# Self-attention heads in two row halves of TensorE, and value products in two column halves, in a decoder layer

## What is computed

```python
q = x @ W_q; k = x @ W_k; v = x @ W_v
latent = (k + v) @ W_down_kv
k_rec, v_rec = latent @ W_up_k, latent @ W_up_v      # 16 heads of 8
scores = einsum('bhqd,bhkd->bhqk', q, k_rec) / sqrt(128)
scores = scores * exp(-0.01 * |t_q - t_k|)
x = x + (softmax(scores) @ v_rec) @ W_o
```

## Time and profile before

| | us |
|---|---|
| median of 3 runs | 535.52 (535.09 to 536.34) |
| profiled execution, device time | 537.88 |
| its span, first to last instruction | 536.1 |
| PE busy | 494.6 (92%) |
| DVE busy | 361.3 (67%) |
| ACT busy | 335.9 (63%) |
| POOL busy | 170.6 (32%) |

### The profile page before, as it was taken

How to read it: one execution, slowest core, us unless ns; L and a number is a source line. 1 busy time by engine, 2 the same in 40 slices (tenths; PEclk the granted TensorE clock), 3 DMA queues, 4 the chain that set the end, 5 groups by cost and what they waited for, 6 DMA issues and landing times.

```text
span 536.1 us, 9771 instructions
## 1 busy us (share of the span) xinstructions
PE 494.6 (92%) x3480; PEld 320.3 (60%) x3480; DVE 361.3 (67%) x858; ACT 335.9 (63%) x659; POOL 170.6 (32%) x292
## 2 busy tenths in 40 slices
PE   7349899999999999997998999999999999999997
PEld 6205433333333333333545998989889898888896
DVE  6889988887878787742436447766666677664345
ACT  4635777878777777787655573837556373647521
POOL 6820023444453544334353312321322322210000
PEclk9857999999999999999898999999999999999999
DMA  8987300034003300003369633424333533400000
GB/s 238 296 253 144 74 17 3 3 76 105 2 2 90 90 2 3 2 4 117 81 187 330 176 93 109 128 61 153 94 119 94 156 97 84 149 19 1 6 6 6
DMA packets 27956, 49.22 MB, mean 92 GB/s; under 512 B 4140, under 2 KB 15860, under 8 KB 27332
## 3 DMA queue, kind: packets, MB, share of 16 engines
q1 hardware_dynamic: 27156, 47.87, 32.3%
q0 software_dynamic: 224, 0.54, 0.4%
q10 hardware_dynamic: 528, 0.18, 0.1%
HBM read 43.67 MB, written 4.72 MB: 90 GB/s over the span
## 4 chain that ended last, share of the span: by engine, by line
PE 71%; DVE 21%; issue 3%; ACT 2%; DMA 1%; POOL 1%; SPq 1%; DVEq 0%; POOLq 0%; ACTq 0%
PE banks L981 48%; PE banks L1090 12%; PE banks L1246 6%; DVE banks L807 6%; DVE logits L883 2%; PE banks L1101 2%; DVE fa L917 1%; DMA operands<-query_parts 1%; DVE fa L913 1%; DVE qc_lo L854 1%; DVE xn L927 1%; DVE f_small L910 1%; DVE fa L918 1%; PE banks L1153 1%; DVE fa L916 1%
## 5 line engine op out<-in xcount | busy, mean ns | idle before, releaser
L672 ACT ACTIVATE probs<-banks 128x512 f32<-128x512 f32 x288 | 160.2, 599 | 50.7 <-PE banks L981 45.2
L807 DVE CUSTOM_DVE_ANT_0 banks<-banks,decay 128x1024 f32<-128x1024 f32 x128 | 155.0, 1244 | 32.4 <-PE banks L981 31.7
L981 PE MATMUL banks<-operands 112*128 112x512 bf16 (+4 forms) x736 | 149.1, 333 | 21.7 <-DMA operands<-query_parts 14.8
L981 PEld LDWEIGHTS banks<-operands 115*128 115x128 bf16 (+1 forms) x736 | 55.4, 98 | 128.0 <-ACT probs L672 55.5
L981 PEld LDWEIGHTS banks<-mem,pT 128*128 128x128 f32 (+1 forms) x816 | 105.5, 191 | 7.5
L981 PE MATMUL banks<-mem,pT 128*128 128x128 f32 (+1 forms) x816 | 109.1, 275 | 0.0
L693 ACT ACTIVATE pT<-banks 128x512 f32<-128x512 f32 (+1 forms) x104 | 60.4, 580 | 52.0 <-PE banks L1246 52.0
L883 DVE CUSTOM_DVE_ANT_0 logits<-banks,mring 128x512 f32<-128x512 f32 (+1 forms) x85 | 56.5, 667 | 27.4 <-PE banks L981 18.6
L535 POOL TENSOR_SCALAR_AFFINE_SELECT probs<-probs 128x128 f32<-128x128 f32 x128 | 37.1, 293 | 111.0 <-ACT probs L672 109.2
L1090 PE MATMUL banks<-probs,v_ext 128*32 128x512 f32 x512 | 68.7, 609 | 0.1
L527 POOL TENSOR_SCALAR mring<-mring 128x1024 f32<-128x1024 int32 (+1 forms) x46 | 43.8, 952 | 62.0 <-DMA mring<-in_mask_BxSxS_ik 60.0
(11 more groups left out here) (169 smaller groups left out, 502.1 us busy)
## 6 DMA issues: line engine op xcount, KB each, us to landing
mring<-in_mask_BxSxS_ik SPq DMA_DIRECT2D x39, 512.0 KB, 3.7
operands<-key_parts SPq DMA_DIRECT2D x24, 192.0 KB
operands<-query_parts SPq DMA_DIRECT2D x21, 192.0 KB
key_parts<-operand_parts SPq DMA_DIRECT2D x10, 256.0 KB, 3.5
mem<-in_ctx SPq DMA_DIRECT2D x3, 832.0 KB, 9.0
mask<-in_mask_BxSxS_ik SPq DMA_DIRECT2D x9, 256.0 KB, 3.0
pT<-in_mask_BxSxS_ik SPq DMA_DIRECT2D x9, 256.0 KB, 3.0
query_parts<-operand_parts SPq DMA_DIRECT2D x4, 384.0 KB, 5.1
```

Source lines behind the costliest of these rows:

```text
L672: act.activation(probs[:, to, :], PS[:, u % 3, :], ACT.Exp).then_inc(s_p, 1)
L807: dve.tensor_tensor_reduce(out=rows, in0=rows, in1=decay[:, off:off + S], scale=1.0, scalar=-3.0e38, op0=ALU.mult, op1=ALU.max, accum_out= ...
L981: return pe.matmul(o, a, b, start=start, stop=stop, skip_group_check=alone)
```

## The change

The shifted copies go: the parts are stored as the six products that count (48 rows), so that the math takes 60 rows and all with the shift 63. Heads 0 and 1 of a group lie in partitions 0 to 62, heads 2 and 3 in 64 to 126. The order of heads in a block changes, so that a score unit and the maximum half next to it in PE's order are mostly in different row halves; a maximum unit is issued as two halves around other work; the ninth score unit is issued as two halves, the second after a semaphore of the first; a value product is issued as two halves of 256 columns with a score unit between them. The spare rows' memsets now cover 128 partitions by half the columns. Stores of key parts are 3 DMAs in place of 5, of query parts 6 in place of 2, loads 2 in place of 3 each.

```diff
--- before.py
+++ after.py
@@ -21,13 +21,14 @@
 LN_EPS = 1e-5
 BLOCK = 16
 PARTS = 3
-SLOTS = 2 * PARTS - 1
-CLEAR_ROW = 64
+SLOTS = PARTS * (PARTS + 1) // 2
 ONES_PAIR = 1.0 + 127.0 * 2.0 ** -16
-MATH_ROWS = 112
-SHIFT_ROW = 112
+ROW_HALF = 64
+MATH_ROWS = 60
+SHIFT_ROW = 60
 FULL_ROWS = SHIFT_ROW + PARTS
 HG = 4
+HH = HG // 2
 VW = 32
 
...
         def operand(buf, which):
-            return ops[buf][:, which, :, :]
+            return ops[buf][:, which, 0:HH, :]
         QL, KL, QU, KU = range(4)
         SPLIT_ORDER = (KL, QL, QU, KU)
         turn_of = SPLIT_ORDER.index
 
         def queries(buf, which, half):
-            return ops[buf][:, which, :, :].rearrange("p h n -> p (h n)").rearrange(
-                "p (a h n) -> p a h n", a=NH, h=HG)[:, half, :, :]
+            return ops[buf][:, which, 0:HH, :].rearrange("p h n -> p (h n)").rearrange(
+                "p (a h n) -> p a h n", a=NH, h=HH)[:, half, :, :]
+
+        KEY_SLOTS = (slice(1, 6, 2), slice(0, 5, 4), slice(2, 3))
+        QUERY_SLOTS = (slice(0, 3), slice(3, 5), slice(5, 6))
+        assert SLOTS == 6
+
+        def row_half(r, rows):
+            return slice(ROW_HALF * r, ROW_HALF * r + rows)
+
+        def max_place(mu):
+            r, m = mu % 2, mu % UNITS // 2
+            return 2 * r + m // TPB, m % TPB
+
...
-            head = i // 2 + 2 * ((i + odd) % 2)
+            head = 2 * (i // 2) + (i + odd) % 2
...
                         sp.wait_ge(ready, NH * (turn_of(w) + 1))
-                        for slot in range(part, SLOTS, PARTS):
-                            sp.dma_start(k_scratch[w // 2, slot].rearrange("d h n -> (d h) n"),
-                                         parts_sb[:, w, part, :]).then_inc(s_scr[w], 16)
+                        to = k_scratch[w // 2, KEY_SLOTS[part]].rearrange("a d h n -> (d h) a n")
+                        sp.dma_start(to, parts_sb[:, w, part, :].unsqueeze(1).broadcast_to(list(to.shape))).then_inc(s_scr[w], 16)
                     return
-                for half in range(NH):
-                    sp.wait_ge(s_lo, NH * turn_of(w) + half + 1)
-                    sp.dma_start(q_scratch[w // 2, half].rearrange("a d h n -> (d h) a n"),
-                                 parts_sb[:, w, :, half * BANK:(half + 1) * BANK]).then_inc(
-                                     s_scr0 if w == QL and half == 0 else s_scr[w], 16)
+                for part, ready in ((0, s_hi), (1, s_mid), (2, s_lo)):
+                    for half in range(NH):
+                        sp.wait_ge(ready, NH * turn_of(w) + half + 1)
+                        to = q_scratch[w // 2, half, QUERY_SLOTS[part]].rearrange("a d h n -> (d h) a n")
+                        src = parts_sb[:, w, part, half * BANK:(half + 1) * BANK]
+                        sp.dma_start(to, src.unsqueeze(1).broadcast_to(list(to.shape))).then_inc(
+                            s_scr0 if w == QL and half == 0 else s_scr[w], 16)
...
-                for s in range(PARTS):
-                    rows = operand(g % NB, w)[s * PARTS * HD:(s + 1) * PARTS * HD, :, :]
+                for r in range(2):
+                    rows = operand(g % NB, w)[row_half(r, SLOTS * HD), :, :]
+                    heads = slice(g * HG + r * HH, g * HG + (r + 1) * HH)
                     if w in (KL, KU):
-                        src = k_scratch[w // 2, s:s + PARTS, :, g * HG:(g + 1) * HG].rearrange("a d h n -> (a d) h n")
+                        src = k_scratch[w // 2, :, :, heads].rearrange("a d h n -> (a d) h n")
                     else:
                         rows = rows.rearrange("p h n -> p (h n)").rearrange("p (a m) -> p a m", a=NH)
-                        src = q_scratch[w // 2, :, :, :, g * HG:(g + 1) * HG].rearrange("f a d h n -> (a d) f (h n)")
+                        src = q_scratch[w // 2, :, :, :, heads].rearrange("f a d h n -> (a d) f (h n)")
                     sp.dma_start(rows, src).then_inc(s_op0 if g == 0 and w == KL else s_op[w // 2][g % NB], 16)
...
                     for i in range(PARTS):
-                        row = queries(g % NB, w, half)[SHIFT_ROW + i:SHIFT_ROW + i + 1, :, :]
-                        sp.dma_start(row.rearrange("p h (t q) -> p (h t) q", q=P),
+                        rows = queries(g % NB, w, half)[SHIFT_ROW + i:P:ROW_HALF, :, :]
+                        sp.dma_start(rows.rearrange("p h (t q) -> p (h t) q", q=P),
                                      shift_parts[:, i, :]).then_inc(s_sh[hg % 2], 16)
 
...
-                qt = (mu // UNITS) % NH * TPB + mu % TPB
+                hg, (h, j) = mu // UNITS, max_place(mu)
+                qt, col = hg % NH * TPB + j, hg * UNITS + h * TPB + j
...
-            def max_unit(mu):
-                hg, h = mu // UNITS, mu % UNITS // TPB
-                g, qt = hg // NH, hg % NH * TPB + mu % TPB
+            def max_wait(mu):
+                hg = mu // UNITS
+                g = hg // NH
                 if hg >= 1 and mu % UNITS == 1:
                     pe.wait_ge(s_mxd, mu)
...
-                ql, kl = queries(g % NB, QL, hg % NH), operand(g % NB, KL)
-                j = mu % TPB
-                for i in range(NH):
-                    last = mm(PS[:, 4 + 2 * max_slot(mu) + i, :], ql[0:MATH_ROWS, h, j * P:(j + 1) * P],
-                              kl[0:MATH_ROWS, h, i * BANK:(i + 1) * BANK])
-                last.then_inc(s_mx, 1)
+                    pe.wait_ge(s_op[0][0], 16 * 2)
+
+            def max_half(mu, i):
+                if i == 0:
+                    max_wait(mu)
+                hg, (h, j) = mu // UNITS, max_place(mu)
+                ql, kl = queries(hg // NH % NB, QL, hg % NH), operand(hg // NH % NB, KL)
+                rows = row_half(h // HH, MATH_ROWS)
+                ins = mm(PS[:, 4 + 2 * max_slot(mu) + i, :], ql[rows, h % HH, j * P:(j + 1) * P],
+                         kl[rows, h % HH, i * BANK:(i + 1) * BANK])
+                if i == NH - 1:
+                    ins.then_inc(s_mx, 1)
...
+            def diagonal_scores(n, r):
+                u = n * PU + 2 * HG
+                g, b = 2 * n // BLKS, 2 * n % BLKS
+                half = b // NT
+                kt = half * TPB + b % NT // 2
+                d0 = kt % TPB * P
+                if r == 0:
+                    pe.wait_ge(s_p, u - 2)
+                else:
+                    pe.wait_ge(s_dg, n + 1)
+                rows = row_half(r, FULL_ROWS)
+                for h in range(HH):
+                    last = mm(PS[:, u % 3, (r * HH + h) * P:(r * HH + h + 1) * P],
+                              operand(g % NB, KU)[rows, h, kt * P:(kt + 1) * P],
+                              queries(g % NB, QU, half)[rows, h, d0:d0 + P], start=(r == 0 and h == 0), alone=True)
+                last.then_inc(s_dg if r == 0 else s_st, 1)
+
             def scores(n, j):
+                if j == 2 * HG:
+                    diagonal_scores(n, 1)
+                    return
...
+                    return mm(bank[:, cols],
+                              operand(g % NB, ks)[row_half(h // HH, FULL_ROWS), h % HH, kt * P:(kt + 1) * P],
+                              queries(g % NB, qs, half)[row_half(h // HH, FULL_ROWS), h % HH, cols], **more)
+                if j % 2 == 1:
                     h, kt, _ = unit(b, j % HG)
...
-            def pv(gb):
+            def pv(gb, between=None):
                 g, b = gb // BLKS, gb % BLKS
                 pe.wait_ge(s_p, gb // 2 * PU + gb % 2 * HG + HG)
                 pe.wait_ge(s_sel, gb // 2 * 5 + gb % 2 * 2 + 2)
                 if b % NT == 0 and gb > 0:
                     pe.wait_ge(s_ot, gb // NT)
-                for i in range(HG):
-                    h, kt, _ = unit(b, i)
-                    last = pe.matmul(PS[h * VW:(h + 1) * VW, 3, :], v_ext[:, kt, g * HG + h, :],
-                                     probs[:, (gb % 2) * HG + i, :], start=(b % NT == 0), stop=(b % NT == NT - 1),
-                                     skip_group_check=True)
+                for q in range(2):
+                    if q == 1 and between is not None:
+                        between()
+                    cols = slice(q * BANK // 2, (q + 1) * BANK // 2)
+                    for i in range(HG):
+                        h, kt, _ = unit(b, i)
+                        last = pe.matmul(PS[h * VW:(h + 1) * VW, 3, cols], v_ext[:, kt, g * HG + h, :],
+                                         probs[:, (gb % 2) * HG + i, cols], start=(b % NT == 0 and q == 0),
+                                         stop=(b % NT == NT - 1), skip_group_check=True)
                 last.then_inc(s_pv, 1)
...
-            def max_turn(mu):
+            def max_turn(mu, steps=range(NH)):
 
                 behind = mu % UNITS if mu >= UNITS else UNITS
                 if behind == 1 and mu < NG * NH * UNITS + UNITS:
-                    max_rows(mu // UNITS - 1)
+                    if 0 in steps:
+                        max_rows(mu // UNITS - 1)
                     return
```

(66 more changed lines are left out.)

9 lines of the change are left out of this document (4 added, 5 removed).

## The result

The changed kernel takes 554.6 us (median of 4 runs, 551.2 to 557.1) against 535.9 of the kernel before (4 runs, 535.1 to 537.0): a ratio of 1.0345, 95% interval 1.0317 to 1.0372. The forecast was 540, with a range up to 554. The profiled execution of after took 557.1 (span 555.4), 2.5 over its median, as that of before stood 2.4 over the median of its first three runs; so the two traces are compared directly.

What follows compares the result with a forecast made beforehand. PE was taken to set the pace in the self-attention pairs, DVE's row maxima from 48 to 62 us. Terms -1 (pairs) +2.5 (before them) +3 (late pairs) +0 (start) = +4.5 on the median 535.5 gave 540, range 519 to 554.

Steps and rivals of the forecast that it cites:

- Before the pairs +2.5 (bounds 0 and +4.5): Maximum units 8 to 22 among 128-row transposes: steps grow from 1.13 to about 1.4, PE becomes the bound, +2.5 us.
- +0.28 for two mode changes: Price of PE's trip between 60-row units and 128-row transposes, read from six matmuls of which two have 4 rows.
- The pairs: -1 forecast: 26 self-attention pairs with maxima: four pairs take 26.1 us against 26.25, over 6.5 such groups -1 us.
- mxd0: First half of a pair's fourth maximum, before the second value product; forecast to wait for its bank until 3.99 us.
- the second wait after a split: In the pair after the split, the second of two maxima issued before s1 (second score unit) waits for its bank: +1.5 us.
- The late pairs: +3 forecast: Last six pairs, without maxima: halved products and mode changes cost 7.7 us, about half covered, +3 (bounds 0 to +7.5).
- the full 7.7: Uncovered late-pair price: 23 places of 0.25 us between score units and 128-row work, plus 4x0.48 for halved products.
- The start: 0 forecast: Up to PE's first maximum: more store bytes, +2.3 us, against earlier stores and better spread loads; 0, between -2 and +2.5.
- No overlap: Rival: row halves do not overlap on PE, the pair takes 6.8 us, +17 over the forecast, 557; chance 18%.
- the faster rival: Mxd0 doesn't wait, its bank being free in time; pair 5.5 us, total 523, or 517 without mode costs; chance 32%.

Runs made afterwards that it cites:

- x1_first_full: Changed kernel with the first 23 maximum units reading 124 rows (both halves) instead of 60: 545.5 us, ratio to before 1.0185.
- x_before_64: Kernel before, with its first 23 maximum units reading 64 of their 112 rows: 542.6 us, ratio 1.0128.
- x4_order: Changed kernel with the first half of each pair's fourth maximum moved behind the second value product: 535.9 us, ratio 1.002.
- x5_both: Changed kernel with first 23 maximum units over 124 rows and first half of each pair's fourth maximum behind the second value product: 528.8 us, ratio 0.9872.
- x_before_72: Kernel before, with its first 23 maximum units reading 72 of their 112 rows: 537.0 us, ratio 1.0014.
- x11_late_full: x6_whole with the scores of the last four pairs taken over 127 rows: 516.3 us, ratio 0.9648.
- x7_same_half: x5_both with every maximum half in the same row half as the score unit beside it, so they can't overlap: 544.1 us, ratio 1.0175.
- x6_whole: x5_both with value products in one piece, each followed by the score unit that stood between its halves: 522.0 us, ratio 0.9738.
- x8_grouped: x4_order with two 60-row maximum units in a row, then two chunks' transposes, ahead of the first pair: 532.2 us, ratio 0.9933.
- x9_exact: x8_grouped with whole value products, every maximum again of one head (60 rows): 527.4 us, ratio 0.984.
- x12_before_64_grouped: x_before_64 with two maximum units, then two chunks' transposes, at a time: 542.0 us, ratio 1.0145.
- x10_only_whole: Changed kernel with only its value products made whole again: 543.9 us, ratio 1.0168.

## Why the prediction was wrong

**Where the miss lies.** The traces are 19.2 us apart, the forecast had 4.5. Of the 14.7 between, 6.2 lie in the pairs (+5.2 for -1), 5.4 before them (+7.9 for +2.5), some 2 in the start of the profiled execution, 0.7 after self-attention and 0.2 in the late pairs. Two terms failed, each in its own way.

**The step that failed by its mechanism is "Before the pairs +2.5 (bounds 0 and +4.5)".** It took +0.28 for two mode changes, and that price held: 0.30 at the low clock, steps of 1.35 and 1.49 at the full one. But it kept the clock of before, with three steps at the low one. In after some eight of these steps, not three, ran at 1.2 GHz (17.5 us, 45.7 to 63.2), at 2.0 to 2.43 each, and the term measured +7.9. An estimate of the parts: 8x0.30 = 2.4 is the mode changes, the other 5.5 the low clock, at which PE and no longer DVE is the bound. x1_first_full (-9.1) and x_before_64 (+6.9 with that alone) confirm from both sides that these rows are the cause. That the change could move the clock was not among the bounds. The Trainium skill (TensorE: Matmul & The Clock Gate, Part 1) says that the gate follows how busy PE has been; here the profile has PE busy 4.00 us of 4.00 at 0.50 from 48 to 60, so a full PE in this view was no sign of a clock about to rise. The 0.28 itself was in part luck: in before's trace the four starts around its two 4-row matmuls (321.25, 321.45, 321.66, 321.86) are each 0.20 to 0.21 apart in place of 0.11, also the two that have the same mode, so that row doesn't isolate entering and leaving.

**The pairs: -1 forecast, +5.2 measured. The steady part was right.** Pair 6.21 (forecast 6.15), four pairs 26.16 (26.1), the wait at mxd0 in each pair, the second wait after a split (+1.32 for +1.5), the value half at 0.57 (0.56), full overlap of neighbours: all as worked out; two small errors in the pair and the split cancel. x4_order shows what mxd0's place costs, 1.7 in four pairs of the steady part and more at the start. What failed is that the steady four were taken for all 6.5 groups. The first eight pairs take 57.5 us where two steady groups take 52.3. Two short stretches of low clock (83.7 to 87.1, 114.4 to 117.8) can hold at most 3.4 of those 5.1. The rest is in the trace at the full clock: three times in these pairs, and nowhere later, DVE has four small operations on weight matrices (turnT, L834 to L838, 1.2 us) between two maxima, at 80.50, 96.41 and 109.83, and mxd0 then waits 1.26, 1.01 and 1.30 where it waits 0.17 to 0.28 in other pairs, together 2.9 more. The first of them:
```profile
80.50 0.55 DVE L834 TENSOR_REDUCE turnT<-wg_raw 128x24 f32<-128x384 f32 x1
...
81.72 1.23 DVE L825 CUSTOM_DVE_ANT_0 banks<-banks,decay 128x1024 f32<-128x1024 f32 x1
```
```profile
83.06 0.39 PE L999 MATMUL banks<-operands 60*128 60x512 bf16 x1 [1.26 <-DVE row_max L825]
```
With PE waiting for DVE in every pair, such work moves PE. x1_first_full has the same long start (57.8), while x5_both, with the same operations but without that chain, takes 49.6 against the 49.0 of two steady groups. No run takes the small operations out by themselves.

**The late pairs: +3 forecast, +3.2 measured, but by luck.** Before had one stretch of low clock here (255.2 to 258.6), after had none. x_before_72, whose late part is that of before, had none either and takes 33.5 from pair 28 to the last exp, where after takes 38.6: at equal clock the price is about 5, two thirds of the full 7.7, not half. (The 7.7 counts the halved products of four pairs; its own text has six without maxima.) x11_late_full puts at least 3 of it on the modes (6.5 less in elapsed time, of which the clock can be 3.4).

**The start: 0 forecast.** About 1 us early in the variants, within the bounds (-2 to +2.5); the profiled execution of after was 2 late, with its stores issued 2.7 later than in x5_both behind a stretch of low clock.

**The rivals.** "No overlap", 557, is near the measured time, and its mechanism is refuted: x7_same_half shows what its absence costs, 15.3. A time that fits is no proof of its reason. The premise of the faster rival, that mxd0 doesn't wait, is false in after; its pair length, 5.5, is near what x4_order has once that wait is moved (5.65 to 5.9 in the steady part). The rival named for x6_whole, that ACT starves when products are whole, is false: over the pairs alone ACT waits 25.4 us for PE there and 29.5 in x5_both. It is PE's weight loads that wait longer for ACT's probabilities (57.4 against 28.7), so with a faster PE more of the pace is ACT's.

**Left open.** What makes the clock stay low. Every traced kernel with 60 or 64 rows before single transposes rose at 58.9 to 65.0, those with full rows, or 72, at 43.0 to 47.7, the grouped ones at 46.7 to 51.7. The number of mode changes, or the pauses they make, is one explanation, rows left unused another. x8_grouped and x9_exact change both at once, and x12_before_64_grouped, which could tell them apart, is inconclusive. Why whole products bring a low clock in the late pairs (x10_only_whole, x9_exact) was not tried.

## What to carry to other kernels

Price a new tile mode at both clocks: where short units in a half-array mode alternate with full-array work at a place where the clock has yet to rise, the later rise can make the cost three times that at the full clock (7.9 us here for 2.5 worked out). Check a steady period against the first periods, where other work is mixed in (5.1 us here). Put a matmul that waits for a bank behind independent work rather than ahead of it; on an in-order engine its wait is paid by all that is queued (18.7 us here). Splitting an instruction group to slip another between its halves pays only if something was starving; two entries into a tile mode cost 7 to 11 us here.

## What the runs showed of the hardware that was not expected

A bf16 matmul over 64 rows behaves differently from one over 72 with no tiling asked for: +6.9 us for the kernel with 64, no change with 72, and 0.30 us for each step between full-array transposes at the same clock. The granted clock stayed at 1.2 GHz for some 37.5 us in after (25.6 to 63.2), in the last 15 of which PE counts as busy without a gap. Two matmuls in different row halves start 3 to 7 ns apart, and a 512-column one beside another costs nothing that the trace can show.
